# Softmax attention in windows of twelve key tiles: value products of two tiles side by side, expert up products among the last steps

## The reference, cut to what matters

```python
x = x + tanh(g_xattn[0]) * linear_attention(layernorm(x), ctx, ctx, mask)       # stage 1
x = x + tanh(g_ffn[0])   * bit_linear_ffn(layernorm(x))                         # "chain", per pair of sequences
x = x + tanh(g_xattn[1]) * softmax_attention(layernorm(x), ctx, ctx, mask)      # stage 2, 16 heads of 8
x = x + tanh(g_ffn[1])   * mixture_of_experts(layernorm(x))                     # stage 3, 8 experts, top 2
# softmax_attention
scores  = einsum('bhqd,bhkd->bhqk', qh, kh) / sqrt(8)
attn    = softmax(scores, axis=-1)
context = einsum('bhqk,bhkd->bhqd', attn, vh)
# mixture_of_experts, for every expert e with gate weight p_e
h = gelu(x @ w1[e].T + b1[e]);   y = h @ w2[e].T + b2[e];   out += p_e * y
```

## Time and profile before

| | |
|---|---|
| median of 3 runs | 747.47 us (747.16 to 750.23) |
| profiled execution | 745.49 us |
| its span, first to last instruction | 743.7 us |
| mean granted clock of TensorE | 0.967 of full |
| TensorE matmul busy | 665.1 us (89%) |
| VectorE, ScalarE, GpSimd busy | 520.3, 513.1, 269.6 us |
| stage 1 and what leads over | up to about 224 us |
| stage 2, 16 windows | about 224 to 626 us |
| stage 3 | about 633 to 743 us |

### The profile page before, as it was taken

How to read it: one execution, slowest core, us unless ns; L and a number is a source line. 1 busy time by engine, 2 the same in 40 slices (tenths; PEclk the granted TensorE clock), 3 DMA queues, 4 the chain that set the end, 5 groups by cost and what they waited for, 6 DMA issues and landing times.

```text
span 743.7 us, 19382 instructions
## 1 busy us (share of the span) xinstructions
PE 665.1 (89%) x7302; PEld 467.0 (63%) x7315; DVE 520.3 (70%) x1236; ACT 513.1 (69%) x839; POOL 269.6 (36%) x324
## 2 busy tenths in 40 slices
PE   3499999986468999999999999999999986999997
PEld 3488888874225665666665666566666664577777
DVE  5788989888778779878978878878876751212112
ACT  4488888876326887887787787787887866634441
POOL 4299999992243214304322422432233100000000
PEclk9899999999589999999999999999999999799999
DMA  4122223345523476356537636644664480211110
GB/s 145 41 84 84 83 87 111 111 142 31 121 73 84 98 167 139 95 129 135 130 91 148 149 91 143 135 110 110 135 157 114 86 192 9 60 29 58 29 42 26
DMA packets 59379, 74.42 MB, mean 100 GB/s; under 512 B 35320, under 2 KB 40178, under 8 KB 59306
## 3 DMA queue, kind: packets, MB, share of 16 engines
q1 hardware_dynamic: 59306, 73.39, 41.8%
HBM read 32.35 MB, written 1.40 MB: 45 GB/s over the span
## 4 chain that ended last, share of the span: by engine, by line
PE 43%; DVE 16%; issue 7%; ACT 2%; POOL 2%; SPq 1%; another core or an unknown queue 1%; DMA 1%; DVEq 0%; POOLq 0%; ACTq 0%
DVE mx L1615 8%; PE ps L662 8%; PE ps L750 7%; PE ps L811 7%; PE ps L823 7%; PE ps L737 6%; PE ps L648 4%; PE ps L654 2%; DVE kvall L1446 2%; ACT P L1023 1%; PE ps L684 1%; DVE amax L1485 1%; POOL KP L1134 1%; DVE silu L1530 1%
## 5 line engine op out<-in xcount | busy, mean ns | idle before, releaser
L1023 ACT ACTIVATE P<-ps,kbias,kscale 125x896 f32<-125x896 f32 x192 | 210.3, 1098 | 86.0 <-PE ps L737 83.0
L1615 DVE TENSOR_REDUCE mx<-ps 128x1 f32<-128x500 f32 x336 | 214.0, 671 | 46.6 <-PE ps L662 44.8
L662 PE MATMUL ps<-KP,Qb 128*128 128x500 bf16 x336 | 128.9, 386 | 16.4 <-DVE mx L1615 10.3
L1134 POOL TENSOR_TENSOR KP<-kvall,KP 128x1500 bf16<-128x1500 f32 x16 | 48.6, 3036 | 230.6 <-ACT KP L966 230.6
L750 PE MATMUL ps<-P,Vp 125*32 125x112 f32 x3072 | 113.5, 265 | 2.8 <-ACT P L1023 1.5
L750 PEld LDWEIGHTS ps<-P,Vp 125*32 125x32 f32 x3072 | 67.4, 109 | 53.1 <-issue 37.8
L533 PE MATMUL ps<-wkv,cT 128*125 128x256 f32 x384 | 91.8, 383 | 1.1 <-ACT arena L901 1.1
L533 PEld LDWEIGHTS ps<-wkv,cT 128*125 128x125 f32 x384 | 69.3, 190 | 10.1 <-issue 1.4
L1084 ACT ACTIVATE arena<-ps,b 128x448 f32<-128x448 f32 x64 | 40.4, 633 | 47.4 <-PE ps L811 41.5
L737 PE MATMUL ps<-QS,KS 128*128 128x112 bf16 x768 | 68.8, 215 | 2.4 <-DVE QS L1621 1.4
L737 PEld LDWEIGHTS ps<-QS,KS 128*128 128x128 bf16 x768 | 55.0, 99 | 23.3 <-issue 3.9
(11 more groups left out here) (216 smaller groups left out, 1007.4 us busy)
## 6 DMA issues: line engine op xcount, KB each, us to landing
cT<-ctxT_dram SPq DMA_DIRECT2D x32, 750.0 KB, 4.2
KS<-KP SPq DMA_DIRECT2D x48, 375.0 KB, 7.3
arena<-KP SPq DMA_DIRECT2D x48, 375.0 KB, 7.2
QS<-QD SPq DMA_DIRECT2D x96, 28.0 KB, 5.7
wgu<-w_dram SPq DMA_DIRECT2D x8, 256.0 KB, 3.2
silu<-w_dram SPq DMA_DIRECT2D x8, 256.0 KB, 2.9
x<-xh_dram SPq DMA_DIRECT2D x1, 512.0 KB, 3.6
mixed<-att SPq DMA_DIRECT2D x16, 28.0 KB
```

The lines of the kernel that those rows point to most:

```text
L662: ins = nc.tensor.matmul(ps[:, bank, 0:KCW], q[:, 128 * c:128 * c + 128], KP[par][0][:, KCW * k:KCW * k + KCW], start=True, stop=True)
L1023: nc.scalar.activation(P[t % 2][0:TK, :].rearrange("p (k n) -> p k n", k=2), src, ACT.Exp, scale=kscale[0:TK, bass.ds(n, 1)], bias=kbias[0 ...
L1134: nc.gpsimd.tensor_tensor(KP[par][2][:], krest, KP[par][1][:], ALU.subtract).then_inc(sem("kp3_ready"), 1)
L1615: ins = v.tensor_reduce(mx[:, c, k:k + 1], ps[:, bank, 0:KCW], AX.X, ALU.max)
```

## The change

Four things are changed; the second follows from the first.
- `weigh` is issued for two tiles at once: on even t for the tiles t-2 and t-1, at t = 0 for the last two tiles of the window before. On odd t there is none. The units keep their places. In the last window (`apart`) `weigh` stays alone, one tile at a time, except for the pair at its t = 0.
- `P` gets four buffers, the two new ones in a free part of `arena`, and the waits of `Exp` and `weigh` go by four.
- The first four `up` products of expert 0 and the logits of all sequences but the last two stand between the last `weigh`, `OT`, `FT`, `FO` and `ET`. `up` (and Gelu) now runs over the first half of the rows in all four blocks of 128, then over the second half, so that the first four need only the first four pairs of sequences.
- The logits go into bank 4 instead of 6. The first `down` waits until VectorE has read them.

```diff
-        P = [sb(f"P{n}", [128, HQ]) for n in range(2)]
+        P = [sb(f"P{n}", [128, HQ])[:] for n in range(2)]
+        P += [arena[:, PAT + HQ * n:PAT + HQ * n + HQ] for n in range(2)]
...
+                apart = fixed(i) and w == B - 1
                 for t in range(T):
                     scores(at, t, 0, first)
                     units_at(t, 0)
                     scores(at, t, 1, first)
                     units_at(t, 1)
-                    if t > 0:
+                    if t == 0:
+                        if not first:
+                            for before in range(T - TOGETHER, T):
+                                weigh(w - 1, 1 - par, before, first_pair)
+                    elif apart:
                         weigh(w, par, t - 1, first_pair)
-                    elif not first:
-                        weigh(w - 1, 1 - par, T - 1, first_pair)
+                    elif t % TOGETHER == 0:
+                        for before in range(t - TOGETHER, t):
+                            weigh(w, par, before, first_pair)
                     units_at(t, 2)
...
+            def up(e, par, first, of=range(8)):
+                xv = xT[:].rearrange("p (b q) -> p b q", q=HALF)
+                for u in of:
+                    k, c = divmod(u, FC)
+                    if u == 0:
+                        pe.wait_ge(sem(f"w1_in{par}"), loads(e, par))
+                    if not (first and u < 4):
+                        pe.wait_ge(sem("h_ready"), 8 * e + u - 3)
...
+            pe.wait_ge(sem("side_free"), emptied((NT - 1, 1), "ET"))
+            up(0, 0, True, range(0, 1))
             fill(AFTER, "OT", B - 1, 1)
-            for unit in LAST:
-                fill(AFTER, unit, NT - 1, 1)
+            up(0, 0, True, range(1, 2))
+            fill(AFTER, "FT", NT - 1, 1)
+            logits(range(0, 3))
+            fill(AFTER, "FO", NT - 1, 1)
+            up(0, 0, True, range(2, 4))
+            logits(range(3, NT - 1))
+            fill(AFTER, "ET", NT - 1, 1)
             pe.wait_ge(sem("side_free"), emptied(AFTER, "ET"))
+            logits(range(NT - 1, NT)).then_inc(sem("logit_ps"), 1)
...
                     if not first:
                         pe.wait_ge(sem("moe_done"), 2 * e + k - 3)
+                    elif par == 0 and k == 0:
+                        pe.wait_ge(sem("logit_ready"), 1)
...
-                if not (first and t < 2):
-                    act.wait_ge(sem("pv_done"), n - 1)
+                if not (first and t < 4):
+                    act.wait_ge(sem("pv_done"), n - 3)
```

More of the change, by code:

```diff
@@ L50 @@
 KSW = NPAIR * S2 + 128 - TK
+PAT = 6016
 MXS = [f"MX{n}" for n in range(CH * KC)]
@@ L73 @@
 CHAIN_PAIRS = NT - 2
+TOGETHER = 2
 EARLY_SIDE = ["K0", "K1", "K2", "AT.0", "V0", "V1", "G.0", "U.1", "V2", "HT.0", "HT.1", "LT.0", "Q1.0", "K0'", "K1'",
@@ L750, in weigh @@
                     ins = nc.tensor.matmul(ps[r:r + PW, 7, c:c + PAIRW], Vp[par][0:TK, t, p, :],
-                                           P[t % 2][0:TK, PAIRW * p:PAIRW * p + PAIRW],
+                                           P[t % 4][0:TK, PAIRW * p:PAIRW * p + PAIRW],
                                            start=(t == 0 and p < 4), stop=(t == T - 1), skip_group_check=True)
@@ L790, in _ @@
             weigh(B - 1, 1, T - 1, False)
-            fill(AFTER, "OT", B - 1, 1)
-            for unit in LAST:
-                fill(AFTER, unit, NT - 1, 1)
-            pe.wait_ge(sem("side_free"), emptied(AFTER, "ET"))
[L797 to L812, removed]
+            def up(e, par, first, of=range(8)):
[6 more added lines that the diff above has]
+                        pe.wait_ge(sem("h_ready"), 8 * e + u - 3)
+                    nc.tensor.matmul(ps[:, u % 4, 0:8 * S], w1_sb[par][:, 128 * c:128 * c + 128],
+                                     xv[:, 8 * k:8 * k + 8, 0:S], start=True, stop=True).then_inc(sem("up_ps"), 1)
@@ new lines, in logits @@
+            def logits(tiles):
+                for t in tiles:
+                    ins = nc.tensor.matmul(ps[:, 4, E * t:E * t + E], xT[:, 128 * t:128 * t + 128], gw_sb[:],
+                                           start=True, stop=True)
+                return ins
+            pe.wait_ge(sem("side_free"), emptied((NT - 1, 1), "ET"))
+            up(0, 0, True, range(0, 1))
+            fill(AFTER, "OT", B - 1, 1)
+            up(0, 0, True, range(1, 2))
+            fill(AFTER, "FT", NT - 1, 1)
@@ L838, in second_biases @@
                 ins.then_inc(sem("b2_ps"), 1)
-            up(0, 0, True)
+            up(0, 0, True, range(4, 8))
             def pair2(i):
@@ L1018, in exponentials @@
                 act.wait_ge(sem("sc_ready"), n + 1)
-                if not (first and t < 2):
-                    act.wait_ge(sem("pv_done"), n - 1)
+                if not (first and t < 4):
+                    act.wait_ge(sem("pv_done"), n - 3)
                 act.wait_ge(sem("kb_ready"), 1)
                 src = ps[0:TK, 2 * (t % 2):2 * (t % 2) + 2, 0:HQ2]
-                nc.scalar.activation(P[t % 2][0:TK, :].rearrange("p (k n) -> p k n", k=2), src, ACT.Exp,
+                nc.scalar.activation(P[t % 4][0:TK, :].rearrange("p (k n) -> p k n", k=2), src, ACT.Exp,
                                      scale=kscale[0:TK, bass.ds(n, 1)],
@@ L1079, in inner @@
                 for u in range(8):
-                    c, k = divmod(u, 2)
+                    k, c = divmod(u, FC)
                     act.wait_ge(sem("up_ps"), 8 * e + u + 1)
@@ L1757, in _ @@
             dve.wait_ge(sem("logit_ps"), 1)
-            lg = ps[:, 6, 0:NT * E].rearrange("p (t e) -> p t e", e=E)
+            lg = ps[:, 4, 0:NT * E].rearrange("p (t e) -> p t e", e=E)
             full3 = [128, NT, E]
```

## The result

| | before | after |
|---|---|---|
| median of 20 runs each, in turns | 745.83 us | 750.85 us (748.72 to 751.96) |
| profiled execution | 745.49 us | 751.06 us |
| its span | 743.7 us | 749.2 us |
| first SH to the last value product (start to start) | 403.45 us | 410.22 us |
| the last value product to the end of the span | 117.95 us | 115.38 us |

The ratio is 1.0047, with a 95% interval from 1.0033 to 1.0061: slower by a little. (It is taken over all runs; the means, 746.89 and 750.40 us, give the same 1.0047, the two medians 1.0067.) The forecast was 747.4 us and no change. Of the 20 executions with the change nine took 748.7 to 749.7 us at a mean granted clock of 0.970 and eleven 750.8 to 752.0 us at 0.965 to 0.969; the profiled one is of the second group.

The account below looks back on a forecast made before the run. A pair of windows was taken as bound by TensorE in some steps, VectorE in others. Stage 2 +5.3 us and its end -5.4 gave -0.1, 745.4 us, stated as 747.4 for the runs' median; range 740 to 753.

Parts of the forecast that it names:

- What a join is worth: Two joined `weigh` on TensorE: each join saves 0.24 us, 90 joins, 21.6 us if every one pays.
- The rival with 1.04: The second joined `weigh` costs all of 0.52 us, a join saves only 0.10; total 753 us, chance 0.10.
- K2 to FT, SH to scores, MX2 to AT: TensorE distances on losing `weigh` cover: 2.02, 1.82, 1.58 us; new waits 0.9 (with LT), 0.7, 0.6 per pair.
- Sum of new waits 4.0 us per pair: Stage 2: TensorE's waits per pair of windows go from 3.9 to 7.9 us, against 2.9 saved; pair 1.1 longer.
- `MX8`, `MX12`: Maxima waiting for reductions behind a chain piece on VectorE: 0.6 us more each, 1.2 per pair.
- the bank rule: A maximum starts no sooner than 1.17 us after the one two before; with others, 0.6 us new wait per pair.
- The rest of stage 2: Outside pairs 1 to 5: pair 0 -0.4 us, windows 12 and 13 -0.5, windows 14 and 15 +0.7.
- The fifth up 5.4 us earlier: End of stage 2: the fifth up follows the first Gelu at 636.3 instead of 641.7, so -5.4 us.
- Granted clock 1.0 throughout: Sign at the end of stage 2: no fall of TensorE's clock, despite 2.9 us waiting for the first Gelu.
- The sum: Whole kernel: stage 2 +5.3 us and its end -5.4 give -0.1; no measurable change, chance 0.50.
- The rival "the clock stays low at the end": Clock falls before FO, moved ups and logits take double, the end's 5.4 us vanish: +5, 752.4 us, chance 0.17.
- The rival "the joins pay": New waits are half those forecast, stage 2 is 5 us shorter, the end 5.4: 737 us, chance 0.23.

Follow-up runs that it names:

- the GpSimd edit: The change, with GpSimd's `last_deviation` (which makes `rstd`) moved ahead of the third key part and query products: 748.37 us, ratio 1.0014 to the kernel before.
- the four profiles with 3.4 us: End alone (0.9947), pairs ahead of the units of place 1 (1.0053), GpSimd's deviation earlier (1.0014), one pair at each window's end (0.9999); ratios to the kernel before.
- one up late: Kernel with one pair at each window's end, plus the fourth up moved behind the last logit product: 746.52 us, ratio 0.9987 to the kernel before.
- two ups late: Kernel with one pair at each window's end, plus the third and fourth ups behind the last logit product: 745.19 us, ratio 0.9974 to the kernel before.
- the joins alone: The change with the end of stage 2 put back as before, joined value products kept: 753.76 us, ratio 1.0069 to the kernel before.

## Why the prediction was wrong, point by point

- **What a join is worth: right.** 0.90 to 0.91 us for a pair, against 0.90. The rival with 1.04 falls: at these products, four column quarters with the same 125 rows, weight loads busy for 0.73 us and products busy throughout fit into 0.91, so the loads did run beside products in flight. The rule that would give 1.04 is in the Trainium skill, TensorE: Matmul & The Clock Gate, section "The mechanism": weight loads overlap products in flight only when the row groups differ. This trace does not agree.
- **K2 to FT, SH to scores, MX2 to AT: right**, each within 0.05 us.
- **"Sum of new waits 4.0 us per pair": too small, the first step that failed.** If every join saved its 0.24, the middle pair lost 1.48 + 12 x 0.24 = 4.4. The term that was missing is GpSimd's `rstd`, a row that the walk left out; with that link taken off the path the pair is 54.0. The other terms of the sum (`MX8`, `MX12`, the bank rule) I have not checked one by one. Over pairs 1 to 5 it is +6.8 instead of +5.5; the GpSimd edit takes back 1.1 of the 1.3.
- **The rest of stage 2: near in its sum (0.0 instead of -0.2), by luck, and not in its parts.** Pair 0 lost nothing, -0.4 as forecast. Windows 12 and 13 came out 0.3 longer instead of 0.5 shorter, windows 14 and 15 together equal instead of 0.7 longer. The first is explained in part by the same link (window 13 gains 1.1 from the GpSimd edit). In the second, window 14 is 1.1 longer, and the wait for the query DMAs behind it is 1.84 us instead of the 2.59 of the earlier trace rows: it took most of the lateness in. That is read from the trace, and I have not tested it.
- **"The fifth up 5.4 us earlier": right**, 5.3.
- **"Granted clock 1.0 throughout": the step that failed most.** I argued from 2.59 us idle in window 15, which had not lowered the clock, and put the danger before FO, where the moved ups did keep it up. It fell in the wait after the last logit, for 6.8 us at a price of 2.8 (1.7 to 2.0 in the four profiles with 3.4 us). That this wait brings the fall is shown for the order of the change: with the wait taken away and the four ups left in place, the clock holds behind the last logit in three profiles (in one of them it falls 13.6 us later, within the first `down`). It is not the only stretch that can: with one up late the clock fell ahead of this wait, and with two ups late there was no such wait, and it fell behind the 1.7 us ahead of ET. That the row in window 15 was no evidence is shown too: behind the same wait of 2.59 us the clock did fall in the kernel with pairs at the window's end and two ups late.
- **The sum.** +5.3 - 5.4 became +6.8 - 2.6. Two errors of 1.5 and 2.8 us, both to the same side, made a change that was to break even slower by half a per cent. (The 2 us that I added for the median of three runs were scatter: over twenty the kernel before has 745.83. And the hand-over in the bank rule is 0.05 us by its rows, not 0.06, which changes nothing.) The rival "the clock stays low at the end" had the right kind of loss, in the wrong place and with a price of 5 us instead of 2.8. The rival "the joins pay" is refuted by the joins alone at 1.0069.

## What to carry to other kernels

A product that seems to be only cost may be the cover of another engine's chain: before it is moved, go through every engine that must finish meanwhile, the one with the least work too, since its row may stand behind an operation that came late. An idle stretch of TensorE ahead of dense work can cost twice, itself and the clock behind it (here 2.8 us, and 1.7 to 2.8 more). Work moved into it helps, but look at the gap that it leaves where it came from. Measure the two halves of a change apart: here one was worth keeping.

## What was unexpected of the hardware

- A 128x128 scaling on VectorE took 1.78 us instead of 0.34 when it met a GpSimd operation of 1.69, and both ended within 0.07 us. One shift of the order brought both together in each of the five middle pairs of windows.
- The same wait for DMAs in window 15 lets the granted clock fall in some profiled executions (behind 2.48, 2.59, 2.69 and 2.73 us) and not in others (behind 2.52, 2.59, 2.61, 2.64 and 2.69). The length of the wait alone does not tell.
- The same code, with the same wait of 2.81 us, had a low clock for 3.4 us in four profiles and for 6.8 in that of the change, 0.8 to 1.1 us apart at the end. With two ups moved into the wait, ups followed the last logit product without a gap and the end was 1.4 us shorter, but the clock fell all the same.
